# Adding the output bias to the x rows on GpSimd instead of multiplying it in on TensorE

## What is computed

```python
# x: 1 x 4096 x 512, ctx: 1 x 3202 x 512, 16 heads of 32, 8 experts, 2 of them per token
q = (layernorm(x) @ Wq + bq); k = (ctx @ Wk + bk); v = (ctx @ Wv + bv)     # split in heads
A = softmax(q k^T / sqrt(32)); out = A v
x = x + (out @ Wo + bo)                      # bo: 512 numbers, the output bias
w = top2(softmax(layernorm(x) @ Wr^T + br))
x = x + sum_e w_e * (layernorm(x) @ We^T + be)
```

## Time and profile before

| | |
|---|---|
| median of 3 executions | 2355.64 us (2354.8 to 2356.03) |
| profiled execution, its own time | 2361.31 us |
| its span, first to last instruction | 2358.5 us |
| mean granted TensorE clock | 0.983 of full |
| TensorE busy | 2266.8 us, 96% |
| VectorE busy | 2035.5 us, 86% |
| ScalarE busy | 1840.5 us, 78% |
| GpSimd busy | 746.6 us, 32% |

### The profile page before, as it was taken

One profiled execution on the slowest core, in us unless ns is written; L12 is line 12 of the kernel. 1 busy time (PEld: TensorE's weight loads), 2 busy tenths in 40 slices (PEclk: granted clock), 3 DMA queues, 4 the chain that ended last, 5 costly groups with the idle time before them and its releaser, 6 DMA issues. The chain is left out here.

```text
span 2358.5 us, 49254 instructions
## 1 busy us (share of the span) xinstructions
PE 2266.8 (96%) x19600; PEld 1088.8 (46%) x19600; DVE 2035.5 (86%) x1830; ACT 1840.5 (78%) x2123; POOL 746.6 (32%) x823
## 2 busy tenths in 40 slices
PE   8999799999999999999999999999999999789998
PEld 7878533333333333333333333333333357578776
DVE  4358579999999999999999999999999988866555
ACT  3213299999999999999999999999999956534332
POOL 2213223323223322223323232332233222245664
PEclk9999899999999999999999999999999999889999
DMA  7436463444464455557444535645434467634463
GB/s 261 166 133 224 171 184 91 109 107 107 113 175 108 127 127 131 130 140 208 109 109 115 120 92 129 170 100 120 109 95 106 109 171 267 201 112 139 144 215 120
DMA packets 145020, 334.24 MB, mean 142 GB/s; under 512 B 32758, under 2 KB 65494, under 8 KB 127644
## 3 DMA queue, kind: packets, MB, share of 16 engines
q0 software_dynamic: 47104, 194.30, 33.8%
q1 hardware_dynamic: 95356, 129.20, 16.8%
q10 hardware_dynamic: 2336, 7.60, 1.0%
HBM read 131.16 MB, written 82.78 MB: 91 GB/s over the span
## 5 line engine op out<-in xcount | busy, mean ns | idle before, releaser
L1162 ACT ACTIVATE probs<-psum 128x1536 f32<-128x1536 f32 x800 | 1159.5, 1449 | 0.0
L1316 PE MATMUL psum<-probs,v_st 128*32 128x512 f32 x6400 | 853.9, 606 | 0.2 <-ACT probs L1162 0.2
L1267 PE MATMUL psum<-q_st,k_st 32*128 32x512 f32 x9600 | 781.2, 426 | 28.6 <-ACT probs L1162 13.6
L1267 PEld LDWEIGHTS psum<-q_st,k_st 32*128 32x128 f32 x9600 | 399.0, 184 | 722.8 <-ACT probs L1161 376.3
L1227 DVE TENSOR_TENSOR even_sums<-even_sums,probs 128x2048 f32<-128x2048 f32 x288 | 659.7, 2291 | 39.1 <-ACT probs L1162 36.2
L1227 DVE TENSOR_TENSOR odd_sums<-odd_sums,probs 128x2048 f32<-128x2048 f32 x256 | 585.4, 2287 | 1.6 <-ACT probs L1162 1.6
L1161 ACT ACTIVATE probs<-psum 128x512 f32<-128x512 f32 x800 | 478.2, 598 | 47.3 <-PE psum L1267 42.8
L1316 PEld LDWEIGHTS psum<-probs,v_st 128*32 128x32 f32 x6400 | 126.1, 108 | 291.3 <-issue 281.9
L2103 PE MATMUL psum<-we_hi,wo 128*128 x624 | 216.9, 409 | 4.5 <-DVE wo L1994 2.5
L977 POOL DMA_DIRECT2D pile<-probs x96 | 88.8, 925 | 247.2 <-DMA pile<-probs 156.7
L956 POOL CAST rest_split<-rest_probs 72x512 fp32r<-72x512 f32 x32 | 37.4, 1169 | 386.1 <-ACT rest_probs L1130 386.1
(11 more groups left out here) (225 smaller groups left out, 2358.9 us busy)
## 6 DMA issues: line engine op xcount, KB each, us to landing
pile<-probs POOLq DMA_DIRECT2D x128, 1024.0 KB, 7.3
token_rows<-rows SPq DMA_DIRECT2D x8, 1028.0 KB, 6.7
xn<-in_x SPq DMA_DIRECT2D x16, 512.0 KB, 6.4
qh_scratch<-o_hi SPq DMA_DIRECT2D x8, 1024.0 KB, 4.5
ql_scratch<-o_lo SPq DMA_DIRECT2D x8, 1024.0 KB, 7.6
q_st<-qh_scratch SPq DMA_DIRECT2D x32, 256.0 KB, 3.0
q_st<-ql_scratch SPq DMA_DIRECT2D x32, 256.0 KB, 3.6
token_rows<-in_x SPq DMA_DIRECT2D x8, 1024.0 KB, 10.7
```

What stands on the lines that cost most here:

```text
L1162: act.activation(probs[:, p, 1:HG, :], psum[:, bank(it, t, 1):bank(it, t, 1) + HG - 1, :], ACT.Exp, bias=-WIDEST, scale=SCALE).then_inc(ex ...
L1267: return nc.tensor.matmul(psum[:, bank(it, t, h), :], k_st[rows, part, t * P:(t + 1) * P], q_st[it % 2][rows, of, :], start=start, stop=stop)
L1316: mm = nc.tensor.matmul(psum[h * DH:(h + 1) * DH, bank, :], lhs(h), rhs(h), start=start, stop=stop)
```

## The change

The bias is loaded into all 128 partitions of a tile `bo_all` and stays unrounded. GpSimd adds it in place to each x tile when that has arrived, and the residual add on VectorE waits for this addition (semaphore `x_biased`) instead of for the load. The bias product, its selector tile, the memsets, the rounding on ScalarE and the subtraction on GpSimd are deleted.

```diff
-        bo_pair = sb("bo_pair", [P, D + P], F32R)
+        bo_all = sb("bo_all", [P, D], F32)
...
     terms = [(j, A, W) for j in range(NG) for A, W in ((hi, wo_hi), (hi, wo_lo), (lo, wo_hi))]
-    bo, picks = g["bo_pair"][:, 0:g["D"]], g["bo_pair"][:, g["D"]:]
-    pe.matmul(psum[:, bank, :], picks, bo, start=True, stop=False)
     for t, (j, A, W) in enumerate(terms):
-        mm = pe.matmul(psum[:, bank, :], A[:, j, :], W[:, j, :], start=False, stop=t == len(terms) - 1)
+        mm = pe.matmul(psum[:, bank, :], A[:, j, :], W[:, j, :], start=t == 0, stop=t == len(terms) - 1)
...
-                pool.memset(bo_pair[:, D:].bitcast(F32), 0.0).then_inc(picks_filled, 1)
-                pool.wait_ge(picks_filled, 1)
-                for r in (0, DH):
-                    pool.memset(bo_pair[r:r + 1, D:].bitcast(F32), 1.0).then_inc(picks_filled, 1)
-                pool.wait_ge(picks_filled, 3)
...
-                    if it == 2:
-                        pool.wait_ge(bo_high_ready, 1)
-                        pool.tensor_tensor(bo_pair[DH:2 * DH, 0:D], bo_raw[DH:2 * DH, :], bo_pair[DH:2 * DH, 0:D].bitcast(F32), ALU.subtract).then_inc(wo_lo_ready, 1)
-                        pool.wait_ge(wo_lo_ready, 2)
...
-                        if it == 1 and t == BO_TILE:
-                            act.wait_ge(small_in, 48)
-                            act.activation(bo_pair[:, 0:D], bo_raw[:], ACT.Copy).then_inc(bo_high_ready, 1)
...
-                pe.wait_ge(wo_lo_ready, 2)
+                pe.wait_ge(wo_lo_ready, 1)
...
+                def add_bias(i):
+                    if i < NTL:
+                        pool.wait_ge(x_in[i % RING], 16 * (i // RING + 1))
+                        pool.tensor_tensor(xb[i % RING][:], xb[i % RING][:], bo_all[:], ALU.add).then_inc(x_biased, 1)
+
+                pool.wait_ge(small_in, 48)
                 for n in range(RING):
                     load_piece(n)
+                add_bias(0)
...
+                add_bias(1)
                 for i in range(2, NTL + 1, 2):
+                    add_bias(i)
                     split_low(pool, i - 1, we_lo_pool)
                     for n in (i + 1, i + 2):
                         if n < NE * KT:
                             load_piece(n)
+                    add_bias(i + 1)
...
                     dve.wait_ge(wo_mm, i + 1)
-                    dve.wait_ge(x_in[i % RING], 16 * (i // RING + 1))
+                    dve.wait_ge(x_biased, i + 1)
```

14 lines of the change are left out of this document (6 added, 8 removed).

## The result

The changed kernel is slower: 2367.4 us in the median of 6 runs (2363.9 to 2369.1) beside 2356.9 us (6 runs, 2354.8 to 2359.1) for the kernel before, ratio 1.0044 with a 95% interval of 1.0032 to 1.0056. That is 10.5 us more, where +1.5 was forecast, and above the range.

What follows compares the result with a forecast made beforehand. TensorE was taken as the bound, VectorE close behind. Rounding -0.5, other parts 0, routing cycles +1.0 and stage start +1.0 gave +1.5 us, so 2357.1 us from the runs' median of 2355.64; range 2349 to 2366.

Steps and rivals of the forecast that it cites:

- What TensorE saves: Projection and routing stage: without the bias product 0.233 us less per tile, cycle of four tiles 15.03 us, 7.2 us over 31 tiles.
- What VectorE can give: Same stage: VectorE's own cycle is 14.3 us, so TensorE stays the bound up to 0.7 us of lock waits per cycle.
- What the added operation costs VectorE: Same stage: GpSimd's additions bring lock waits to 1.8 us per cycle, VectorE's cycle to 16.1 us, the stage +1.0 us.
- the bound of 1.16 us for one instruction: Most that one GpSimd addition was taken to cost VectorE at the SBUF port: 1.28 - 0.12 us.
- the placing: Four additions placed in the cycle from 1974.11: two cost nothing, one about 0.35 us, one about 1.2.
- The start of the stage: First x tile's addition delays VectorE's normalising product, the first residual add following 0.95 us late; +1.0 us, 0 to +1.3.
- Other parts: Attention and waits outside the main terms, each near nothing; ScalarE's rounding -0.5 us, GpSimd's subtraction 0.
- GpSimd's subtraction of 3.23 us in iteration 2: Attention: it slowed one VectorE addition to 3.38 us from 2.28; removing it worth nothing, hidden by VectorE's slack.
- ScalarE's rounding: Attention: removing ScalarE's rounding of the bias, 0.63 us long, was worth -0.5 us (0 to -0.63).
- rival C: Routing stage: additions come too late, residual adds wait about 1 us every second tile, +6 us after the lost gain; chance 0.05.
- the signs in the profile: Stage: VectorE busy about 1.5 us more per cycle, only in two-SBUF-input forms, small ones above 1 us; waits for ScalarE nearly gone.
- rival B: Routing stage: VectorE becomes the bound with 2.8 us of lock waits per cycle, cycle 17.1 us, 2364.6 us; chance 0.27.

Runs made afterwards that it cites:

- run 1: The changed kernel without the 32 GpSimd additions, the output bias left out of the result; ratio 0.9969 to the kernel before.
- run 7: The changed kernel with each addition from tile 2 on waiting until VectorE begins residual add and statistics; ratio 1.0020 to the kernel before.
- run 14: The kernel of run 1 plus two statistics (0.69 us each) computed a second time per cycle on VectorE; ratio 0.9994 to the kernel before.
- run 2: The changed kernel with additions in place but writing where nobody reads, the residual waiting for the x load alone; ratio 1.0049 to the kernel before.
- run 10: The changed kernel with each GpSimd addition waiting until the one before it is complete; ratio 1.0071 to the kernel before.
- run 4: The changed kernel with a weight load put ahead of each addition, so additions come one by one; ratio 1.0077 to the kernel before.
- run 11: The changed kernel with a one-column GpSimd memset, and a wait for it, ahead of each addition; ratio 1.0040 to the kernel before.
- run 5: The kernel before with only the rounding of the bias moved from ScalarE to GpSimd in iteration 2; ratio 1.0004 to the kernel before.
- run 9: Bias added by accumulating DMAs instead of engine additions, x copies in attention iterations 25 to 28, accumulations in 26 to 29; ratio 1.0007 to the kernel before.

## Why the prediction was wrong, by its own steps

**What TensorE saves**: right. 15.03 us per cycle forecast, 15.03 measured (run 1), so 0.233 per tile and not 0.31.

**What VectorE can give**: right in form. Forecast: own cycle 13.55 + 0.76 = 14.3 us, bound above 0.7 us of holds. Measured: rest 0.79 instead of 0.76, own work about 13.2 (13.76 less 0.53 held, run 1), so an own cycle of 14.0. The single cycles of runs 7 and 14 show the rule itself, busy time plus a constant.

**What the added operation costs VectorE: the step that failed.** It took 1.8 us of holds per cycle; the changed kernel has 3.1. Put into the prediction's own formula, 14.3 + 3.1 = 17.4, less the 0.3 by which the own cycle was taken too long, this is near the measured mean of 16.94, in which three of six cycles are TensorE's. For the stage the step had given +1.0 us over 7.5 cycles; measured were +5.87 in six cycles and +2.3 behind them. Two things in the step were wrong. First, the bound of 1.16 us for one instruction: it assumed that VectorE gets the port when the addition ends, and that an addition takes it when its record begins. Runs 2 and 10 and the trace after show that the next addition can take it again (3.54 without a gap, 2.33 with one), and that a subtraction begun 0.49 us ahead of an addition's record was held in nine of twelve cases. Second, and worth more, the placing: the prediction found two of four additions a free place by following one cycle, and left GpSimd's weight subtractions at their old 0.25. In the changed kernel GpSimd's additions follow the weight loads, which wait for VectorE's weight subtraction (30.0 us in 15 times from 1924 to 2044), and behind that subtraction stand the small two-input chains. Where each falls is not a matter of chance in run 4, where each cycle meets the same chain. Runs 10 and 11 shortened the longest holds and kept their sum, and neither was faster than the changed kernel beyond its interval; so the length of the single hold is not what sets the time.

**The start of the stage**: right. The normalising product took 1.64 instead of 0.69 us, as forecast (+0.95), and the part ahead of the cycles is 1.3 us longer; two small operations that were held 3.0 us there (L1695, L1697) were not in the forecast, so that the number is near in part by luck. **The end of the stage** was left out of the sum; it is 2.3 us longer. Of this 1.5 are one hold at its edge (2043.98, 1.70 us for 0.17), and the later holds are 0.3 longer than before; the rest stays open. A smaller surprise stands in the sixth cycle: TensorE waits 2.90 us until 2038.36, and the granted clock is 0.73 and 0.84 in the stretches of 4 us from 2036 and 2040, so part of each is at 1.2 GHz. Twelve products took 4.36 us instead of 3.04. VectorE is the bound there (rest 0.90 instead of 0.79), so little of it can show in the time:

```profile
2036.00:2040.00 4.00, 1.64 (x4) 1.38 (x5) 3.90 (x6) 2.06 (x5) 2.94 (x3) 0.73 0.35 106
2040.00:2044.00 4.00, 4.00 (x21) 2.48 (x20) 3.76 (x15) 0.00 (x0) 0.23 (x1) 0.84 0.17 60
```

```profile
2038.36 4.36 PE L759 MATMUL psum<-wo,q_st 128*128 128x512 f32 x12 [2.90 <-DVE q_st L750]
```

**Other parts**: GpSimd's subtraction of 3.23 us in iteration 2 was worth nothing, as forecast (50.13 us with and without). ScalarE's rounding was given -0.5; run 5 finds no gain, with an interval that still holds -0.5. That residual adds would not wait (against rival C) is right, by the trace and by run 2. Of the signs in the profile, VectorE's waits for ScalarE did go (1.1 us of 11.5 are left) and the small forms did reach above 1 us; but VectorE's busy time rose by 2.4 us per cycle, not 1.5, and not only in forms with two SBUF inputs: five conversions of indices took 0.57 or 0.58 us instead of 0.17.

**The rivals**: what happened is rival B, VectorE the bound with 2.8 us of holds and 2364.6 us, 2.8 us under the measured median. It was right on the mechanism and nearly on the size (2.8 of 3.1), and partly on the place: its meeting of GpSimd's weight subtraction with the projection-side subtraction occurs (2030.19, 1.66 us), but most of the 9.1 us for which L750 was held in the six cycles came from additions. It had a chance of 0.27, and the range ended just past its point, at 2366, with no room for holds longer than the bound of 1.16; the trace before has no two GpSimd port users in a row from which to take one.

## What to carry to other kernels

Where VectorE is within a microsecond of the bound, a GpSimd instruction that reads SBUF is VectorE work: count what it holds against VectorE's busy time, and start from the number of two-input and small instructions that it can meet, not from a free place found by hand. Judge such a change by VectorE's busy time per cycle plus its constant rest, not by the longest hold or by how busy GpSimd is. An operand that has to be added can be had without any engine's arithmetic by accumulating DMAs in an earlier stage, if they are spread thin and keep out of the stretches that reload.

## What the runs showed of the hardware that was not expected

- Two GpSimd additions in a row can hold a VectorE instruction through both (3.54 us for one of 0.69, in the changed kernel and run 2); a wait for the first one's completion between them lets it in (2.33). They need not: of the same pairs an operation of 0.17 us begun 0.8 us behind the first's record ran between the two (0.50). A weight load's issue between two additions is no such gap (3.14 us for 0.17 in run 4). The Trainium skill (SBUF — State Buffer, section Who interferes with whom) has whoever issues first keep the ports for its whole instruction; 3.54 is more than one instruction.
- Behind a weight load's issue an addition held VectorE's subtraction although that had begun 0.49 us ahead of the addition's record, nine times of twelve at that lead. The issue itself does not hold it (0.69 us under it in run 11). What decides stays open.
- Eight columns are as dear as 512: held instructions of 0.17 us took 1.26 (run 7) and 1.68 (run 4).
- A memset of GpSimd, behind which no two-input instruction was held, holds VectorE's conversion of integers (0.91 us instead of 0.17). A weight subtraction of GpSimd holds a one-input operation too (0.85 instead of 0.17 in run 7).
- Eight accumulating DMAs of 256 KB in one iteration of the attention cost it up to 4.2 us (run 9), although no engine uses their data there: a DMA issued just ahead of them landed in 12.4 and 13.1 us (7.7 in the median before), and ScalarE and TensorE waited for it. One or two cost nothing outside the reloads (50.13 us).
- After a wait of 1.7 to 1.9 us in iteration 1 TensorE's granted clock fell to 1.2 GHz for 3.4 us in four executions and stayed at 2.4 GHz in thirteen; with the fall the iteration was 1.4 to 1.9 us longer.
